# Matrix products of zeros at the start of a two-layer kernel, ahead of the first transposes and of the first product

## What is computed

```python
# x: (8, 256, 1024) f32; mask: (8, 1024, 1024) int32, here all ones; W0, W1: (1024, 1024); coeff: (8,)
def layer0(x):
    sign = 2 * mask - 1
    return einsum('bsi,oi->bso', x, W0) + b0 + einsum('bsi,bio->bso', x, sign) * coeff[:, None, None]
def layer1(x):
    A, B = lora_A[ids], lora_B[ids]                # rank 16, one adapter for each of the 8 batches
    return einsum('bsd,od->bso', x, W1) + b1 + (x @ A^T) @ B^T
x = x + layer0(x)
x = x + layer1(x)
```

## Time and profile before

| | us |
|---|---|
| median of 3 runs | 438.1 |
| lowest and highest run | 437.32 and 438.97 |
| the profiled execution, its own time | 438.86 |
| its span in the profile | 437.1 |
| PE busy, share of the span | 405.9, 93% |
| DVE busy | 286.0, 65% |
| ACT busy | 235.9, 54% |
| POOL busy | 14.0, 3% |

### The profile page before, as it was taken

How to read it: one execution, slowest core, us unless ns; L and a number is a source line. 1 busy time by engine, 2 the same in 40 slices (tenths; PEclk the granted TensorE clock), 3 DMA queues, 4 the chain that set the end, 5 groups by cost and what they waited for, 6 DMA issues and landing times.

```text
span 437.1 us, 5483 instructions
## 1 busy us (share of the span) xinstructions
PE 405.9 (93%) x2033; PEld 339.5 (78%) x2033; DVE 286.0 (65%) x334; ACT 235.9 (54%) x350; POOL 14.0 (3%) x26
## 2 busy tenths in 40 slices
PE   0586999788999999999999999999999999999996
PEld 0474888566888888888888888888888888888884
DVE  1717656787678765886588767876588658865512
ACT  1727667546445755656556644575565555665412
POOL 1212020000000000000000000000000000000000
PEclk9996999999999999999999999999999999999999
DMA  8698399345963299237922595329823692254002
GB/s 197 194 314 258 91 248 241 96 86 162 212 144 97 76 226 197 66 97 177 232 77 83 162 221 134 96 80 232 189 66 97 155 250 81 82 162 114 1 0 97
DMA packets 92542, 63.29 MB, mean 145 GB/s; under 512 B 3547, under 2 KB 86499, under 8 KB 92516
## 3 DMA queue, kind: packets, MB, share of 16 engines
q1 hardware_dynamic: 92516, 62.95, 57.2%
HBM read 51.39 MB, written 8.39 MB: 137 GB/s over the span
## 4 chain that ended last, share of the span: by engine, by line
PE 85%; SPq 4%; DVE 4%; ACT 2%; DMA 2%; issue 2%; ACTq 0%
PE ps L591 25%; PE ps L618 13%; PE ps L617 13%; PE ps L593 13%; PE ps L619 13%; PE ps L601 3%; PE ps L577 3%; DMA wm<-in_mask_Bx4096x_ik_dram 2%; PE ps L629 2%; SPq L234 1%; SPq L190 1%; DVE wlo L473 1%; SPq L192 1%; ACT w1hi L325 1%; DVE wm L467 1%
## 5 line engine op out<-in xcount | busy, mean ns | idle before, releaser
L591 PE MATMUL ps<-xhl,whi 128*128 128x512 f32 x512 | 187.6, 405 | 4.3 <-DVE wlo L473 3.5
L593 PE MATMUL ps<-xhl,wlo 128*128 128x256 f32 x512 | 144.9, 283 | 0.0
L591 PEld LDWEIGHTS ps<-xhl,whi 128*128 128x128 f32 x512 | 97.6, 191 | 27.1 <-DVE wlo L473 3.6
L473 DVE TENSOR_TENSOR wlo<-wm,whi 128x1024 fp32r<-128x1024 f32 x64 | 78.4, 1225 | 48.7 <-ACT whi L337 48.7
L337 ACT ACTIVATE whi<-wm 128x1024 fp32r<-128x1024 f32 x64 | 67.8, 1059 | 73.9 <-DVE wm L467 72.7
L617 PE MATMUL ps<-w1hi,yhl 128*128 128x512 f32 x256 | 101.8, 398 | 0.0
L618 PE MATMUL ps<-w1lo,yhl 128*128 128x512 f32 x256 | 100.7, 393 | 0.0
L619 PE MATMUL ps<-w1hi,yhl 128*128 128x512 f32 x256 | 100.5, 393 | 0.0
L593 PEld LDWEIGHTS ps<-xhl,wlo 128*128 128x128 f32 x512 | 98.1, 192 | 2.4
L467 DVE SCALAR_TENSOR_TENSOR wm<-wm,cs,w0t 128x1024 f32<-128x1024 f32 x64 | 81.4, 1273 | 14.1 <-ACT w0t L315 14.1
L330 ACT ACTIVATE wm<-wm 128x1024 f32<-128x1024 int32 x64 | 67.4, 1054 | 8.2 <-DMA wm<-in_mask_Bx4096x_ik_dram 8.2
(11 more groups left out here) (42 smaller groups left out, 168.0 us busy)
## 6 DMA issues: line engine op xcount, KB each, us to landing
wm<-in_mask_Bx4096x_ik_dram SPq DMA_DIRECT2D x64, 512.0 KB, 4.4
xraw<-in_x_dram SPq DMA_DIRECT2D x32, 256.0 KB, 7.1
out_dram<-zst SPq DMA_DIRECT2D x32, 256.0 KB, 2.5
w0raw<-in_L_cond_W_dram SPq DMA_DIRECT2D x8, 512.0 KB, 7.1
w1raw<-_L_cond_base_weight_dram SPq DMA_DIRECT2D x8, 512.0 KB, 6.5
bt<-bhl SPq DMA_DIRECT2D x48, 64.0 KB, 2.9
abraw<-in_L_cond_lora_A_w_dram SPq DMA_DIRECT2D x8, 64.0 KB, 2.6
abraw<-in_L_cond_lora_B_w_dram SPq DMA_DIRECT2D x8, 64.0 KB, 1.8
```

Source lines behind the costliest of these rows:

```text
L473: nc.vector.tensor_tensor(wlo[:, s, :, :], wm[:, n % MS, :].rearrange("p (k o) -> p k o", k=KT), whi[:, s, :, :].bitcast(F32), ALU.subtrac ...
L591: nc.tensor.matmul(ps[:, bank, :], whi[:, s, k, :], xhl[:, b % 2, k, :], start=(k == 0), stop=False, skip_group_check=True)
L593: op = nc.tensor.matmul(ps[:, bank, 0:S], wlo[:, s, k, :], xhl[:, b % 2, k, 0:S], start=False, stop=(k == KT - 1), skip_group_check=True)
```

## The change

A function `spin(count)` issues `count` matmuls of 512 columns on PE. Both operands are parts of bt, which holds zeros at that time, and each result overwrites bank HB, which nobody reads before unit (w0,2,1) is put there. 28 of them stand ahead of the first transposes, and 13 between the transpose of b0row and the first product. PE waits for `consts_set` to reach 1 before the first. The memset of bt is moved to the head of POOL's program, so that this 1 stands for bt. Nothing that is computed changes.

```diff
@@ -283,6 +283,7 @@
+            nc.gpsimd.memset(bt[:, :].bitcast(F32), 0.0).then_inc(consts_set, 1)
             nc.gpsimd.memset(ident[:, :], 0.0).then_inc(ident_set, 1)
             pool.wait_ge(ident_set, 1)
             nc.gpsimd.affine_select(out=ident[:, :], in_=ident[:, :], compare_op=ALU.not_equal, fill=1.0, base=0,
@@ -290,7 +291,6 @@
             pool.wait_ge(ident_set, 2)
             eye_w0(0)
             eye_w0(1)
-            nc.gpsimd.memset(bt[:, :].bitcast(F32), 0.0).then_inc(consts_set, 1)
             nc.gpsimd.memset(ht[:, :].bitcast(F32), 1.0).then_inc(consts_set, 1)
             nc.gpsimd.memset(at[:, :, 2 * P:].bitcast(F32), 0.0).then_inc(consts_set, 1)
             eye_w0(2)
@@ -629,6 +629,13 @@
+            def spin(count):
+
+                for _ in range(count):
+                    nc.tensor.matmul(ps[:, HB, :], bt[:, 0:P], bt[:, HALF:D], start=True, stop=True)
+
+            pe.wait_ge(consts_set, 1)
+            spin(28)
             pe.wait_ge(ident_set, 2)
             turn_unit("w0", 0, 0)
             turn_unit("w0", 0, 1)
@@ -636,6 +643,7 @@
             turn_unit("w0", 1, 1)
             pe.wait_ge(b0_in, 16)
             nc.tensor.transpose(ps[:, TB, 0:KT], b0row[:, :], ident[0:KT, 0:KT]).then_inc(b0_turned, 1)
+            spin(13)
             for n in range(NS + 1):
```

## The result

The changed kernel took 439.5 us (median of 18 runs, 437.2 to 441.6), the kernel before 438.3 us beside it (18 runs, 436.9 to 439.9). The ratio is 1.003 with a 95% interval of 1.0017 to 1.0044: slower by about 1.2 us, which is less than the 0.5% that the prediction took for the least that can be told, but clear of their spread. The profiled execution took 438.8 us, as long as the one of before, so its trace need not hold the loss.

A forecast was written before the change was run, and what follows sets the result against it. PE bounds the kernel behind 44 us; before 37.28 us transfers and ACT's steps set the pace, with 4.4 us of PE idle as cover. Terms summed to 0, so the forecast was the 438.1 us median, range 436.2 to 439.6 us.

The forecast's parts named there:

- The zero tile first: POOL's start: ident is ready 0.95 us later, hidden by POOL's 8.97 us wait for slab 0; cost 0.
- 28 multiplications: PE's start, ahead of the first transposes: 8.9 us of work, ending at 10.7 us, just in time; no term.
- 13 more: PE before the first product: 3.0 to 5.6 us, at worst 0.8 us past the b0col wait, inside 4.4 us cover; 0.
- Products at the upper level: PE, 23.31 to 32.92 us: 2.7 us of PE time vanish, but PE then waits longer for ACT's copy; 0.
- The clock after the gap: PE from 37.28 us: the lower level stays; bounds 2.5 us gained to about 1 us lost; 0 in the sum.
- The transfers: SyncE's early issues: nothing ahead of mask 3's issue waited for PE, so no transfer moves; 0.
- The least that can be told: Whole-kernel time: about 0.5% (2.2 us) is what a measurement can tell from no change.
- A: Lower level sets the pace from 19.69 to 32.92 us: 3.6 us faster, 434.5 us; chance 0.04.
- C: Spins run over at the start, first product about 12.2 us late: 444.6 us, slower; chance 0.05.
- D: Zeros might not raise PE's clock level at the start; the cover still holds: 438.1 us; chance 0.12.
- B: Clock is up at 37.28 us, the lower stretch shrinks or goes: 2.5 us faster, 435.6 us; chance 0.04.

The follow-up runs named there:

- r2: Only the memset of bt moved first, no multiplications of zeros, against the kernel before: 437.6 us, ratio 1.0000.
- r3: The change with only its first 28 multiplications of zeros, without the 13, against the kernel before: 438.0 us, ratio 1.0002.
- r4: The change with only its 13 later multiplications of zeros, without the 28, against the kernel before: 437.7 us, ratio 0.9998.
- r13: Memset of bt first, no spins, 38 matmuls of 8 zero columns ahead of the first transposes, against the kernel before: 439.3 us, ratio 1.0023.
- r15: The change with float32 zeros, spin(7) and spin(3) for spin(28) and spin(13), against the kernel before: 438.0 us, ratio 0.9985.
- r7: The changed kernel itself, one more profiled execution: 438.2 us.
- r5: Memset of bt first, no spins, 8-column matmuls: 24 behind slab 0's transposes, 26 behind b0row's; against the kernel before: 436.4 us, ratio 0.9979.
- r6: The change plus 24 matmuls of 8 columns behind the transposes of slab 0, against the kernel before: 438.6 us, ratio 1.0020.
- r9: Memset of bt first, 16 multiplications of zeros only in PE's wait before slab 3's half 1 transposes, against the kernel before: 436.6 us, ratio 0.9973.
- r11: The change plus the 16 multiplications of r9 in PE's wait, against the kernel before: 438.4 us, ratio 0.9997.
- r1: The changed kernel timed again, against the kernel before: 439.1 us, ratio 1.0034.
- r17: r9 with 4 float32 multiplications of zeros in place of its 16, against the kernel before: 436.5 us, ratio 0.9967.
- r14: r9 plus 38 matmuls of 8 zero columns ahead of the first transposes, against the kernel before: 436.1 us, ratio 0.9954, five executions.

## Why the prediction was right or wrong

The forecast was 438.1 us, no difference. The measured loss is 0.3%, inside the range and inside the 0.5%, but a difference all the same, on the side to which the sum had no term.

- *The zero tile first*: right. The order alone gives 1.0000.
- *28 multiplications*: right, 8.8 us for 8.9, and 8.1 to 9.5 us in the other traces; where the level rises differs, so the 0.1 us is luck. *13 more*: 4.8 us, inside its bounds, the first product at 20.9 us and the cover intact.
- *Products at the upper level*: right, the same work ends 2.5 us further ahead of the transposes, and all of it is lost in the wait for ACT.
- *The clock after the gap*: right. It fell, and the lower stretch behind the wait was 2.8 to 6.1 us long in the six traces of the change, in five of them shorter than in the one trace of before (5.1 us); r2, r3, r4, r13 and r15 have 3.5 to 5.4 us. A second dip, not forecast, stands at 81 to 85 us of the first trace, behind a wait of 1.9 us for DVE, and costs 0.4 us: from 80.3 us to the first finish PE needs 22.4 us where other traces need 21.9. Only two of the six traces have it (the first and r7), and four of other kernels do (r5, r6, r9, r11).
- *The transfers*: **this step failed.** "So no transfer moves" looked only at issues that wait for PE. It left out that PE's instructions come over the same 16 DMA engines, although the page of before had the queue, and although each added matmul is two more instructions. The term should have been: 82 instructions, a first fetch that moves from 39.1 us to between 27.6 and 38.3 us, and 1.07 us where it comes by 28.3 us. That is a part of the loss; the rest of it is open.
- *The least that can be told*, put at 0.5%: wrong, the 18 runs of each told 0.3%.
- *Rivals*: A fell (products 2.5 us sooner, nothing gained), C fell (13 spins in 3.28 us in r1, so 0.24 us from one to the next), D fell (the level rose). B's mechanism is real: with the gap closed or filled the kernel gains 0.2 to 0.3% (r5, r9, r17), by their medians 1.2 to 1.4 us of the 2.5 us that it was put at. But the change lengthens that gap and doesn't close it.

How much of the loss theory F explains stays partly open. Shown are the delay of `sign(3)` in the traces with an early fetch, that 38 multiplications with hardly any columns make the kernel 1 us slower, and that the change's columns in half the instructions cost nothing. But in the six traces of the change the fetch was early enough in two, which gives 2/6 x 1.07 = 0.36 us of 1.2 us. r6, with an issue of 3.08 us, doesn't make it more: from mask 2 to `sign(3)` it took 12.21 us, 1.3 us above the mean of the fourteen. No execution of the change above 440 us was caught in a trace, so whether the rest is rare cases of the fetch, the issues ahead of mask 2, or something else isn't known. r14 speaks against a cost of the instructions in every setting. Nor was a kernel tried in which only the place of the fetch moves and nothing else.

## What to carry to other kernels

In this kernel multiplications of zeros paid in the last gap ahead of the stretch that PE bounds, not at the start: the level that they raised there fell again in the next gap, and the time won before it fell into that gap. Filler is better made of few, large instructions: with half of them the loss was gone (r15), perhaps because instructions at the head of an engine's program bring its next fetch forward, into the transfers that the start waits for. When a step is costed at nothing because no issue waits for it, look as well at what else uses the DMA engines, the instruction queues among it.

## What the hardware showed that was not expected

- One fetch of PE's instructions is one packet of 16 KB on one DMA engine. It held that engine for 0.9 us alone (5.7% of 16 us) and for 1.2 us beside full traffic (3.7% of 32 us), and for 3.0 us in r6 (9.5% of 32 us), where the transfers had just started again.
- The length of the lower stretch differs between executions of one kernel, and the time with it: 437.4 us at a mean granted clock of 0.996, 438.2 us at 0.992 (35 and 83 executions of the kernel before).
- A matmul of 8 columns isn't free: 38 took 8.27 us at the start, 0.22 us each, half of what one of 512 columns takes at the lower level. 24 took 5.26 us in r5 and 3.33 us in r6, behind work at the upper level.
- A float32 multiplication of 512 columns costs as much PE time as four fp32r ones, in two matmul records: four took 3.70 us where 16 took 3.90 us.
